# A two-layer transformer block on one core: operand stacks and quantized-tile turns moved to other slots of a hand-written order

## The reference, cut to what matters

```python
x = L0_attn_x                                   # (16, 512, 128)
xn = _layernorm(x)
x = x + _L0_attn_ref(xn, ...) + _L0_ffn_ref(xn, ...)
xn = _layernorm(x)
x = x + _L1_attn_ref(xn, ...) + _L1_ffn_ref(xn, ...)
```

## Time and profile before

| | |
|---|---|
| median of 3 timed runs | 2108.49 us |
| profiled execution, its own time | 2108.19 us |
| its span, first to last instruction | 2106.2 us |
| PE busy | 1934.5 us (92%) |
| DVE busy | 1540.6 us (73%) |
| ACT busy | 1375.7 us (65%) |
| POOL busy | 1143.8 us (54%) |
| mean granted TensorE clock | 0.981 |

### The profile page before, as it was taken

How to read it: one execution, slowest core, us unless ns; L and a number is a source line. 1 busy time by engine, 2 the same in 40 slices (tenths; PEclk the granted TensorE clock), 3 DMA queues, 4 the chain that set the end, 5 groups by cost and what they waited for, 6 DMA issues and landing times.

```text
span 2106.2 us, 49813 instructions
## 1 busy us (share of the span) xinstructions
PE 1934.5 (92%) x17353; PEld 1264.0 (60%) x17353; DVE 1540.6 (73%) x5223; ACT 1375.7 (65%) x3861; POOL 1143.8 (54%) x1799
## 2 busy tenths in 40 slices
PE   3789999999999999999999999999999999998978
PEld 1455666656566575666657566575656657565645
DVE  6558778687776868778687877868777686876646
ACT  1677585675857667585766858567685766757531
POOL 4676374655637465473746647475563746545220
PEclk9779999999999999999999999999999999999999
DMA  5102021110301102020210201121030110201010
GB/s 146 27 9 44 4 39 23 34 29 8 54 4 38 24 20 42 4 56 6 39 24 18 44 4 39 23 39 24 10 52 4 38 24 17 40 4 34 4 32 6
DMA packets 172653, 59.37 MB, mean 28 GB/s; under 512 B 139643, under 2 KB 169971, under 8 KB 172403
## 3 DMA queue, kind: packets, MB, share of 16 engines
q1 hardware_dynamic: 172403, 56.19, 13.9%
HBM read 14.22 MB, written 4.19 MB: 9 GB/s over the span
## 4 chain that ended last, share of the span: by engine, by line
PE 56%; ACT 16%; DVE 12%; POOL 8%; issue 7%; DMA 1%; SPq 0%; ACTq 0%; DVEq 0%; POOLq 0%
PE ps L1124 11%; PE ps L1260 8%; PE ps L1195 8%; PE ps L1205 7%; ACT ring L946 5%; PE ps L1138 5%; PE ps L1114 4%; ACT pb L955 3%; PE ps L1245 3%; DVE ring L577 3%; PE ps L1183 2%; DVE lin L609 2%; POOL ring L843 2%; PE ps L1103 2%; PE ps L1171 2%
## 5 line engine op out<-in xcount | busy, mean ns | idle before, releaser
L843 POOL TENSOR_SCALAR ring<-ring,row_rcp,tau_row 128x128 f32<-128x128 f32 (+3 forms) x1024 | 625.5, 618 | 676.1 <-DVE row_rcp L584 676.1
L946 ACT ACTIVATE ring<-ring,neg_max 128x128 f32<-128x128 f32 (+3 forms) x1024 | 570.8, 558 | 504.0 <-DVE neg_max L577 499.4
L1124 PE MATMUL ps<-identf,ring 128*128 128x128 f32 x2560 | 378.6, 287 | 10.4 <-POOL ring L843 7.6
L955 ACT ACTIVATE pb<-ps 128x512 f32<-128x512 f32 x640 | 348.0, 583 | 27.5 <-PE ps L1124 23.2
L1124 PEld LDWEIGHTS ps<-identf,ring 128*128 128x128 f32 x2560 | 279.2, 143 | 83.4 <-issue 39.0
L577 DVE CUSTOM_DVE_ANT_1 ring<-ps,bias_t 128x384 f32<-128x384 f32 (+1 forms) x496 | 286.7, 614 | 53.7 <-PE ps L1114 46.4
L1260 PEld LDWEIGHTS ps<-ed_t,h 128*128 128x128 f32 (+1 forms) x1920 | 254.6, 191 | 97.2 <-issue 93.7
L1260 PE MATMUL ps<-ed_t,h 128*128 128x128 f32 (+1 forms) x1920 | 270.6, 277 | 0.0
L1205 PE MATMUL ps<-xn1T,eu_t 128*128 128x512 f32 (+1 forms) x480 | 256.5, 616 | 1.3 <-DVE h L633 1.2
L1195 PE MATMUL ps<-xn1T,eg_t 128*128 128x512 f32 (+1 forms) x480 | 255.6, 614 | 2.2 <-DVE h L626 2.1
L1114 PE MATMUL ps<-qkT 32*128 32x128 f16 (+3 forms) x1024 | 201.4, 308 | 47.1 <-DVE neg_max L577 28.0
(11 more groups left out here) (152 smaller groups left out, 2815.7 us busy)
## 6 DMA issues: line engine op xcount, KB each, us to landing
x_t<-x SPq DMA_DIRECT2D x16, 256.0 KB, 2.9
x<-x SPq DMA_DIRECT2D x16, 256.0 KB, 2.9
o_rows<-o_stack SPq DMA_DIRECT2D x256, 16.0 KB
out<-x SPq DMA_DIRECT2D x16, 256.0 KB, 2.3
qkT<-qkx SPq DMA_TRANSPOSE x128, 3.2
bias_t<-bias SPq DMA_DIRECT2D x1, 1536.0 KB, 7.8
eg_t<-eg SPq DMA_DIRECT2D x1, 860.0 KB
eu_t<-eu SPq DMA_DIRECT2D x1, 860.0 KB
```

Source lines behind the costliest of these rows:

```text
L843: pool.tensor_scalar(e, e, row_rcp[:, m % 2, r:r + 1], tau_row[:, i, HG * g + r:HG * g + r + 1], ALU.mult, ALU.add).then_inc(p_ok.sem, 1)
L946: act.activation(e, e, ACT.Exp, bias=neg_max[:, n % 2, r:r + 1], scale=-1.0, accum_out=row_sum[:, n % 2, r:r + 1]).then_inc(exp_ok.sem, 1)
L955: act.activation(pb[:, c % NPB, :], bank(turn_bank(q)), ACT.Relu).then_inc(t_taken[q % 2].sem, 1)
L1124: last = pe.transpose(o[:, r * P:(r + 1) * P], ring_of(i, r)[:, k * P:(k + 1) * P], idf)
```

## The change

Two edits to the order; no instruction is added or left out.

- The stacks of layer 0 of every batch but batch 0: `stack_high` at slots 10, 14, 15, 18 (from 10, 11, 12, 13), `stack_low` one slot on, the transpose one more. Batch 0 keeps the old slots.
- The turns of the quantized tiles at slots 11, 15, 15, 17 (from 11, 13, 13, 15). They are taken out of `beside` and stand in a loop of their own ahead of it, on PE (behind `turn_probs`), on ACT (behind the scores' work) and in the tickets. So in a slot they come before the work of all four batches.

```diff
-TURN_H, FUTURE_V, FUTURE_Y = (ATT + 11, ATT + 13, ATT + 13, ATT + 15), ATT + 61, ATT + 63
+TURN_H, FUTURE_V, FUTURE_Y = (ATT + 11, ATT + 15, ATT + 15, ATT + 17), ATT + 61, ATT + 63
-TURN_STACK0, TURN_STACK1 = QKV0 + 5, QKV1 + 8
+TURN_STACK1 = QKV1 + 8
+STACK0 = ((10, 11, 12, 13), (10, 14, 15, 18))
-TURNS = (("x", (TURN_X,)), ("xq", (TURN_XQ,)), ("hid", TURN_H), ("xn1", (TURN_X1,)),
+TURNS = (("x", (TURN_X,)), ("xq", (TURN_XQ,)), ("xn1", (TURN_X1,)),
...
+            for b, p in self.beside(f, s):
+                for k in range(T):
+                    if TURN_H[k] == p:
+                        self.turn["hid", b, k] = len(self.turn)
...
-                    if 0 <= p - TURN_STACK0 < T:
-                        turn_stack0(b, p - TURN_STACK0)
+                    if p - 2 in STACK0[b > 0]:
+                        turn_stack0(b, STACK0[b > 0].index(p - 2))
...
-                if 0 <= p - QKV0 - 4 < T:
-                    stack_low(b, 0, p - QKV0 - 4)
+                if p - 1 in STACK0[b > 0]:
+                    stack_low(b, 0, STACK0[b > 0].index(p - 1))
...
-                if 0 <= p - QKV0 - 3 < T:
-                    stack_high(b, 0, p - QKV0 - 3)
+                if p in STACK0[b > 0]:
+                    stack_high(b, 0, STACK0[b > 0].index(p))
...
-                for name, t in at((("hid", TURN_H),), p):
-                    turned(("hid", b, t), hqT[:, t, :, :].rearrange("p c n -> p (c n)"), 3 * P)
...
+                for b, p in plan.beside(f, s):
+                    if p in TURN_H:
+                        for k in range(T):
+                            if TURN_H[k] == p:
+                                turned(("hid", b, k), hqT[:, k, :, :].rearrange("p c n -> p (c n)"), 3 * P)
                 for b, p in plan.beside(f, s):
                     beside(b, p)
...
-                for name, t in at((("hid", TURN_H),), p):
-                    turn_hidden(b, t)
...
+                for b, p in plan.beside(f, s):
+                    if p in TURN_H:
+                        for k in range(T):
+                            if TURN_H[k] == p:
+                                turn_hidden(b, k)
                 for b, p in plan.beside(f, s):
                     beside(b, p)
```

## The result

The changed kernel takes 2123.5 us (2122.64 to 2124.68, four runs) against 2108.76 us for the kernel before in the same comparison: ratio 1.0071, 95% interval 1.0054 to 1.0089. That is slower, clear of noise, and inside the stated range.

The account below looks back on a forecast made before the run. ACT, though 65% busy on average, was taken to bound slots 12 to 19. 1.0 us in each of 14 frames plus 0.5 for frame 0 gave 14.5 on 2108.19, so 2122.7, predicted as 2123 us; range 2106 to 2130.

Parts of the forecast that it names:

- the busiest engine of the whole span: Skill page's rule: improve the engine of highest occupancy; over the whole span PE bounds, ACT's moves are free, 2108.5 us.
- the start of the exp of slot 14: On ACT, set by DVE's row minimum: about 1043.02 in place of 1043.72, so 0.70 us earlier.
- ACT's pause before that of slot 16: The 0.68 us ACT stood before the exp of slot 16, taken as room for part of 1.46 us added work.
- two waits: DVE's 1.32 us before the last `silu` for a tanh; PE's 0.45 us before layer 1's second q/k/v product for `hidden`.
- The last stack ahead of the tanh: ACT, slot 18: `stack_high` of tile 3 stands ahead of the last tanh and costs 0.60 us.
- The copy behind the norm: ACT, slot 17: the third copy of a quantized tile, 0.37 us, making the exp of slot 18 0.45 late.
- TensorE's wait in slot 16 for the copy of tile 1: PE at L1124: the bank is that of tile 1's copy, made by ACT at 1045.03 to 1045.5.
- POOL's subtractions: `stack_low` of tiles 1 to 3 among or behind scalings of 0.85 us each; end in time, POOL having stood 2.41 us.
- what the prediction put at nothing: Gain on DVE's pass and ACT's exp from pulling the four transposes apart: given nothing, at most 0.1 us a frame.
- No change: ACT's lateness behind the norm is taken up; 0.08 us a frame left, 2109.5 us, within 0.2%; chance 0.12.
- Faster: DVE's lead of 0.45 us lives on to the frame's end, 6.3 us gained, 2102 us; chance 0.13.
- Slower still: DVE's `silu` of tile 1 in slot 14 waits for PE's turn in slot 15; 1.5 us a frame, 2130; chance 0.07.

Follow-up runs that it names:

- The last experiment: The kernel before with only the turns' slots changed to 11, 13, 15, 15, inside `beside` as before: 2105.69 us, ratio 0.9977.
- turns alone: The changed kernel with the stacks of every batch back at slots 10 to 13: ratio 0.9984 against the kernel before.
- last stack at 19: The changed kernel with tile 3's stack one slot later (10, 14, 15, 19), behind the last tanh: 2114.1 us, ratio 1.0019.
- stacks alone: The kernel before with only the stack edit (10, 14, 15, 18), turns left as they were: 2122.97 us, ratio 1.0058.

## Why the prediction was right

**The bound.** The claim was that ACT is what the others wait for in slots 12 to 19 though busy only 65% on average. It holds for a part of them. In the changed kernel the two places of one extra copy show it for slot 17 (0.44 us a frame) and show that it isn't so in slot 13 (0.07). By the busiest engine of the whole span both copies would have been free, and the change too.

In the kernel before, ACT is the one only from the exp of slot 16 on. Up to there its chain of work that ended last runs through PE and then DVE:

```profile
1041.13 0.66 PE ps L1213 x6
...
1043.43 0.60 DVE ring L577
...
1046.29 0.03 ACT ring L946
```

Behind the norm it leaves ACT for PE's turn of `xn1` at 1050.07; the path by the last tanh meets it at the second q/k/v product. The last experiment agrees with the first part: one turn less on PE ahead of slot 14 brought 0.25 us a frame. The prediction's sum didn't rest on the wider claim. It took the start of the exp of slot 14 from DVE, and ACT's pause before that of slot 16 from the rows. In the changed kernel the chain runs from the exp of slot 14 to the last tanh through ACT, with casts and copies in it that were not there:

```profile
1050.21 0.80 ACT ring L951 x2
1051.01 0.29 ACT qkx L941
1051.30 0.31 ACT qkx L942
1051.61 0.73 ACT hqT L917 x2
...
1056.60 0.36 ACT hqT L917
...
1058.22 0.29 ACT qkx L941
1058.51 0.31 ACT qkx L942
1058.82 0.37 ACT tanh_t L974
```

That the last tanh carries the frame was argued in the prediction from two waits. All seven kernels bear it out: against the kernel before, the frame grows or shrinks by what that tanh moves, counted from the load of x (in us; to 0.04).

| Kernel | last tanh | frame |
|---|---|---|
| turns at 13, 15, 15 | -0.28 | -0.25 |
| turns alone | -0.15 | -0.13 |
| last stack at 19 | +0.42 | +0.41 |
| stacks alone | +0.80 | +0.81 |
| the change | +0.98 | +0.99 |
| with a copy in slot 13 | +1.02 | +1.06 |
| with a copy in slot 17 | +1.42 | +1.43 |

**Its steps.** The order of the shifts was as forecast, and none was off by more than 0.10 us. The exp of slot 14 was 0.10 earlier than worked out, since the residual add and the score follow each other on DVE in 0.59 us (in place of the 0.68 that I took) and ACT followed the sooner. That is why each later start lies 0.05 to 0.09 under its forecast. The last stack ahead of the tanh was put at 0.60 and gave back 0.58 when it was moved away. The copy behind the norm was put at 0.37: the step after is 1056.84 - 1056.48 = 0.36.

**What lay beside.** TensorE's wait in slot 16 for the copy of tile 1 came as said (1.21 us, and 1.44 for its weight loads). Nothing of the loss is seen to come from it: with that wait in place the kernel with the last stack at 19 loses 0.41, which is the copy behind the norm (0.36) and 0.05 more. No run takes the wait away alone. POOL's subtractions stayed hidden: POOL itself stood 1.38 us for ACT before those of tile 3. The transposes are spread over 15.9 us of SP's queue, and the DMA engines' share in the first stretch fell from 0.85 to 0.12. The exp of slot 14 took 0.72 us in place of 0.74 and DVE's pass ahead of it 0.68 in place of 0.69, so what the prediction put at nothing is some hundredths, if it comes from that at all.

**The frames.** Here the sum was right by terms that cancel. Full cost was forecast for frames 1 to 14, 14.0 us. From the times of the loads and stores on SP, frame 1 pays 127.71 - 127.04 = 0.67, frame 2 125.87 - 125.07 = 0.80, the ten frames behind them 10.01, the last two 1.02 and 1.00: 13.50. Frame 0 pays 0.06 where 0.5 was taken, frame 15 pays 0.35 where nothing was, and behind it 0.70 is given back, in all 13.2 us of span, against 14.5 forecast. The remaining 1.4 us of the 14.6 between the two profiled executions (2122.80 and 2108.19) lies outside the span, 3.4 us against 2.0, and no part of the argument had it. So it is luck that the profiled time met its forecast of 2122.7 to 0.1 us: the span was 1.3 us short and the rest 1.4 us long. The other three runs have 1.8 to 1.9 us outside and spans of 2120.7 to 2122.8. Frame 1 isn't a clean price either, since the granted clock was not full in it (0.97 before, 0.99 after, from 146 to 270 us).

The 0.70 given back has its place: SP's last residual load starts 3.50 us behind the store after, 4.18 before. The load waits for the landing of the store, so the store landed 0.68 sooner. In the six other kernels this distance is 3.80 to 4.29 us, and 3.97 and 4.16 in the two that hold the whole change and a copy more, so it scatters by itself, and the change isn't shown to have brought the 0.68.

**The rivals.** No change: ACT's lateness behind the norm was not taken up by anything; frames 3 to 12 are 1.00 longer each, with the last tanh 0.98 late. Faster: DVE's lead of 0.45 (0.53 measured) does live on, but only without the stacks, as turns alone show; with them it ends at ACT, as argued. Slower still: DVE didn't stand for the turn of tile 1. Its `silu` came at 1049.98, right behind the score of 1049.37.

## What to carry to other kernels

When work is moved inside a repeating order, price it by the queue of the engine in the stretch where it lands, not by the engine's mean load: the same 0.40 us copy cost 0.44 us a frame in one slot and 0.07 in another. Room that an earlier slot gains on an in-order engine is lost if its next instruction waits for somebody else. And a pause can be sold only once, so that two moves that cost 0.81 and -0.13 us a frame by themselves cost 0.99 together. Ask of each candidate slot what stands behind it: one turn moved to a slot with a pause behind it gave 0.25 us a frame, where the full change lost 0.99.

## What the runs showed beside

The start is not as steady as the frames. The first four loads of x show it: in the changed kernel the fourth is at 146.05 us, with the extra copies, which are not in frame 0, at 147.83 and 147.94. The granted TensorE clock between 100 and 146 us was 0.75, 0.69 and 0.73 in these three (a mean over the levels of 1.2 and 2.4 GHz), with PE busy 37.5 to 38.6 of 46 us; from 160 us to the next load it was 1.00. The clock alone doesn't order the loads: with the last stack at 19 it was 0.71, and the fourth load came at 145.88. What makes the difference stays open. Some 1.8 us of a whole run's time come about there, as much as 0.13 us a frame would make in 14 frames.

One frame of every trace is longer than its neighbours, always the one that ends with the load near 1020 to 1034 us: 125.13 us (897.56 to 1022.69) against 124.86 for the one ahead of it (772.70 to 897.56) before, 126.14 against 125.86 after, 125.27 against 124.73 with the turns alone. Its cause is open. The granted clock dips in it in the kernel before (0.84 and 0.82 in the two stretches of 5 us from 935 to 945 us), but it is 1.00 throughout with the stacks alone, where this frame is 125.94 us against 125.68, so such a dip isn't the whole of it. A mean over frames should leave this one out when tenths count, as the one over the last five does.
